# A gated graph network and three graph layers on one core: sums written into PSUM before the convolutions, one accumulator for both gates, GpSimd left with the split of x

## The reference, cut to what matters

```python
h = x                                              # layer 0: gated graph network, 3 steps
for _ in range(3):
    a = adj @ h                                    # in and out matrix are the same here
    av = concat([a, a])
    z  = sigmoid(av @ w3.T + w3_b + h @ u3.T + u3_b)
    r  = sigmoid(av @ w4.T + w4_b + h @ u3.T + u3_b)
    hv = tanh(av @ w5.T + w5_b + (r * h) @ u5.T + u5_b)
    h  = (1 - z) * h + z * hv
x = layernorm(x + h)
rel = adj.T * (q @ k.T)                            # layer 1: relation, rows divided by their norm
x = layernorm(x + (rel / norm(rel)) @ v)
x = layernorm(x + (adj @ x) @ l2_w + l2_bias)      # layer 2: first convolution
x = layernorm(x + (norm_adj @ x) @ l3_w + l3_bias) # layer 3: second convolution
```

## Time and profile before

| | |
|---|---|
| runs | 1341.83, 1343.10, 1343.95 us; median 1343.1 |
| profiled execution, span | 1341.3 us (its time is the span and some 1.8 us around it, by the median) |
| instructions | 21962 |
| PE matmul / weight load busy | 1283.5 us (96%) / 1130.6 us (84%) |
| DVE busy | 1074.2 us (80%) |
| ACT busy | 714.1 us (53%) |
| POOL busy | 530.3 us (40%) |
| granted TensorE clock | full in nearly all slices |

### The profile page before, as it was taken

The page is one execution under the profiler, slowest core; times in us unless marked ns, Lnnn a source line. Parts: engine busy times, 40 slices in busy tenths (PEclk is TensorE's granted clock), DMA queues, the critical chain, the costliest instruction groups (busy, mean ns, idle before and its releaser), DMA issues.

```text
span 1341.3 us, 21962 instructions
## 1 busy us (share of the span) xinstructions
PE 1283.5 (96%) x7912; PEld 1130.6 (84%) x7912; DVE 1074.2 (80%) x2110; ACT 714.1 (53%) x1229; POOL 530.3 (40%) x586
## 2 busy tenths in 40 slices
PE   7899999999999999999999999999999999999995
PEld 6788898888979889898888988889898888988795
DVE  5579788797878968788797887978789687885897
ACT  5655555545555555555555655455555555556541
POOL 1135343443443434443353444443534343441254
PEclk9999999999999999999999999999999999999998
DMA  5010100001000010000001001010000100000000
GB/s 173 1 32 1 40 10 16 31 0 47 0 20 27 0 47 0 31 16 16 31 0 47 0 16 31 0 47 0 31 16 0 47 0 31 16 16 1 1 1 32
DMA packets 29386, 29.19 MB, mean 22 GB/s; under 512 B 2352, under 2 KB 28464, under 8 KB 29360
## 3 DMA queue, kind: packets, MB, share of 16 engines
q1 hardware_dynamic: 27808, 28.32, 6.4%
q0 software_dynamic: 192, 0.52, 0.2%
q10 hardware_dynamic: 1360, 0.01, 0.1%
HBM read 20.45 MB, written 8.39 MB: 22 GB/s over the span
## 4 chain that ended last, share of the span: by engine, by line
PE 75%; DVE 14%; issue 5%; POOL 4%; DMA 1%; ACT 1%; DVEq 0%; ACTq 0%; POOLq 0%
PE b_ps L482 35%; PE f_ps L482 35%; DVE b_a_lo L1352 3%; POOL b_rstd L366 2%; PE f_ps L579 2%; DVE normed L1324 2%; DVE hb_feat L1285 2%; DVE b_a_lo L1259 1%; POOL b_var_eps L364 1%; PE b_ps L579 1%; PE b_ps L596 1%; DMA bias_in<-in_L_gnn_u_b 1%; DVE f_cand L1279 1%; PE b_ps L627 1%; DVE hb_node_lo L1299 1%
## 5 line engine op out<-in xcount | busy, mean ns | idle before, releaser
L364 POOL TENSOR_TENSOR b_var_eps<-b_moments,eps 128x2 f32<-128x2 f32 x120 | 34.6, 288 | 339.4 <-DVE b_moments L1313 339.3
L350 POOL TENSOR_TENSOR f_kept<-f_kept,hf_feat 128x512 f32<-128x512 f32 x66 | 91.0, 1379 | 169.7 <-ACT f_kept L941 169.6
L1324 DVE TENSOR_SCALAR normed<-summed,b_moments,b_rstd 128x256 f32<-128x256 f32 x180 | 96.5, 577 | 6.5 <-POOL b_rstd L366 6.5
L375 POOL TENSOR_TENSOR skip<-normed,bias_out 128x512 f32<-128x512 f32 x60 | 88.1, 1469 | 10.3 <-DVE normed L1324 10.3
L366 POOL TENSOR_TENSOR b_rstd<-b_var_eps,neg_half 128x2 f32<-128x2 f32 x120 | 86.1, 718 | 9.4
L350 POOL TENSOR_TENSOR b_kept<-b_kept,hb_feat 128x512 f32<-128x512 f32 x30 | 45.7, 1525 | 110.5 <-ACT b_kept L941 110.5
L1306 DVE BATCH_NORM_STATS2 b_stats<-summed 128x6 f32<-128x256 f32 x240 | 88.4, 410 | 0.8 <-issue 0.3
L946 ACT ACTIVATE f_cand<-f_ps,bias_c 128x512 f32<-128x512 f32 x66 | 45.5, 690 | 63.8 <-PE f_ps L482 63.5
L890 ACT ACTIVATE f_a_hi<-f_ps 128x512 fp32r<-128x512 f32 x68 | 40.6, 598 | 71.6 <-PE f_ps L482 69.9
L890 ACT ACTIVATE b_rh_hi<-b_ps 128x512 fp32r<-128x512 f32 x90 | 53.6, 596 | 45.4 <-PE b_ps L482 45.4
L482 PE MATMUL f_ps<-adjT_hi,hf_node_hi 128*128 128x256 f32 x264 | 75.8, 287 | 0.3 <-POOL hf_node_lo L338 0.3
(11 more groups left out here) (330 smaller groups left out, 5081.6 us busy)
## 6 DMA issues: line engine op xcount, KB each, us to landing
x_front<-in_x SPq DMA_DIRECT2D x16, 512.0 KB, 3.5
x_back<-in_x SPq DMA_DIRECT2D x15, 512.0 KB, 3.5
out<-result SPq DMA_DIRECT2D x15, 512.0 KB, 3.0
x_back<-in_L_gnn_u_w SPq DMA_DIRECT2D x2, 256.0 KB, 9.2
bias_out<-in_L_gnn_bias POOLq DMA_DIRECT2D x4, 128.0 KB, 6.7
b_z<-in_L_gnn_w_w SPq DMA_DIRECT2D x1, 512.0 KB, 11.6
b_gate<-in_L_gnn_w_w SPq DMA_DIRECT2D x1, 512.0 KB, 12.5
b_kept<-in_L_gnn_w_w SPq DMA_DIRECT2D x1, 512.0 KB, 13.0
```

Source lines behind the costliest of these rows:

```text
L350: pool.tensor_tensor(L.kept[:, k], L.kept[:, k], L.state.feat[:, k], ALU.mult).then_inc(L.s_kept, 1)
L364: pool.tensor_tensor(Y.var_eps[:, g], Y.moments[:, g, :, 1], eps[:], ALU.add).then_inc(Y.s_var, 1)
L375: pool.tensor_tensor(Y.skip[:, g], Y.normed[:, g], bias_out[:, j], ALU.add).then_inc(Y.s_skip, 1)
L1324: last = dve.tensor_scalar(dst[:, g, c], Y.summed[:, g, c], Y.moments[:, g, c, 0:1], Y.rstd[:, g, c:c + 1], ALU.subtract, ALU.mult)
```

## The change

- **Convolutions.** `fill` (DVE) writes normed + bias into ps0 ahead of `convolve`, whose matmuls then all accumulate onto it (start=False). `sum_conv`, `add_bias`, `skip` are gone; for layer norms 2 and 3 `stats_of` and `normalise` read ps0.
- **Gates.** `reset` accumulates w4 a onto ps0 itself; `reset_gate` takes the sigmoid from ps0 with its bias. `update` then adds (w3 - w4) a onto the same ps0, so it waits for the reset sigmoid. `keep_base` and `reset_arg` are gone; the matrix `w3 - w4` costs one subtraction on DVE at the start.
- **1 - z.** `keep_gate` is gone; DVE makes (z - 1) h with one scalar_tensor_tensor, and `new_h` subtracts it.
- **Norms.** The squares are summed on DVE and go to PE as plain fp32, two `pe.matmul` a graph in place of four; `squares_hi`, `squares_lo` are gone.
- **GpSimd** keeps the split of x, `inverse_std` and `inverse_norm`.
- All `body` and `finish` lists are written in a new order.

```diff
-                product(L.ps1[:, k], columns(w4T, k), mixed(L)).then_inc(L.s_reset, 1)
+                product(L.ps0[:, k], columns(w4T, k), mixed(L), start=False).then_inc(L.s_reset, 1)
...
             def update(L, n, k):
-                pe.wait_ge(L.s_a_lo, upto(n))
-                pe.wait_ge(L.s_base_kept, upto(n, k))
-                product(L.ps0[:, k], columns(w3T, k), mixed(L), start=False).then_inc(L.s_update, 1)
+                pe.wait_ge(L.s_r, upto(n, k))
+                product(L.ps0[:, k], columns(w34T, k), mixed(L), start=False).then_inc(L.s_update, 1)
...
             def candidate_mixed(L, n, k):
-                pe.wait_ge(L.s_reset_arg, upto(n, k))
+                pe.wait_ge(L.s_a_lo, upto(n))
...
                 if L is back and later(n):
-                    pe.wait_ge(main.s_sum, ln(n - 1, 3, k))
+                    pe.wait_ge(main.s_normed, ln(n - 1, 3, k))
...
-                pe.wait_ge(Y.s_sq_lo, upto(q, g))
+                pe.wait_ge(Y.s_sq_sum, upto(q, g))
                 for c in range(C):
-                    for part in (Y.sq_hi, Y.sq_lo):
-                        last = pe.matmul(Y.ps1[:, g, 2 * c:2 * c + 2], part[:, g, c * P:(c + 1) * P], ones[:],
-                                         start=part is Y.sq_hi, stop=part is Y.sq_lo, skip_group_check=True)
+                    last = pe.matmul(Y.ps1[:, g, 2 * c:2 * c + 2], Y.sq_sum[:, g, c * P:(c + 1) * P], ones[:],
+                                     start=True, stop=True, skip_group_check=True)
...
             def convolve(Y, q, j, g):
+                pe.wait_ge(Y.s_filled, conv(q, j, g))
                 pe.wait_ge(Y.s_ax_lo, conv(q, j, g))
                 for c in range(C):
                     last = product(Y.ps0[:, g, c * D:(c + 1) * D], graph_columns(Y.y_hi, Y.y_lo, g, c),
-                                   whole((w2s, w3s)[j]))
+                                   whole((w2s, w3s)[j]), start=False)
...
             def reset_gate(L, n, k):
-                act.wait_ge(L.s_reset_arg, upto(n, k))
-                act.activation(L.gate[:, k], L.gate[:, k], ACT.Sigmoid).then_inc(L.s_r, 1)
+                act.wait_ge(L.s_reset, upto(n, k))
+                act.activation(L.gate[:, k], L.ps0[:, k], ACT.Sigmoid, bias=bias_r[:, k:k + 1]).then_inc(L.s_r, 1)
...
+            def keep(L, n, k):
+                dve.wait_ge(L.state.s_feat, upto(n, k))
+                dve.wait_ge(L.s_z, upto(n, k))
+                dve.scalar_tensor_tensor(L.kept[:, k], L.z[:, k], 1.0, L.state.feat[:, k], ALU.subtract,
+                                         ALU.mult).then_inc(L.s_kept, 1)
...
-                dve.tensor_tensor(dst[:, k], L.kept[:, k], L.cand[:, k], ALU.add).then_inc(done, 1)
+                dve.tensor_tensor(dst[:, k], L.cand[:, k], L.kept[:, k], ALU.subtract).then_inc(done, 1)
...
+            def layer_sum(Y, j, g, c):
+                return Y.summed[:, g, c] if j < 2 else Y.ps0[:, g, c * D:(c + 1) * D]
...
-            def sum_conv(Y, q, j, g):
-                dve.wait_ge(Y.s_skip, conv(q, j, g))
-                dve.wait_ge(Y.s_conv, conv(q, j, g))
-                dve.tensor_tensor(Y.summed[:, g], graph_bank(Y.ps0, g), Y.skip[:, g], ALU.add).then_inc(Y.s_sum, 1)
+            def fill(Y, q, j, g):
+                dve.wait_ge(Y.s_normed, ln(q, j + 1, g))
+                dve.tensor_tensor(graph_bank(Y.ps0, g), Y.normed[:, g], bias_out[:, j], ALU.add).then_inc(Y.s_filled, 1)
```

The new order of the body on PE (the calls that moved; f is `front`, b is `back`, 2p is the first and 2p+1 the second step):

```diff
                 update(back, q, 0)
+                for k in range(2):
+                    mix(front, 2 * p, k, p)
                 candidate_mixed(back, q, 0)
                 update(back, q, 1)
                 candidate_mixed(back, q, 1)
                 for k in range(2):
                     candidate_reset(back, q, k)
-                for k in range(2):
-                    mix(front, 2 * p, k, p)
                 base(front, 2 * p, 0)
+                reset(front, 2 * p, 0)
                 turn_h3(main, q, 0)
                 base(front, 2 * p, 1)
+                reset(front, 2 * p, 1)
+                update(front, 2 * p, 0)
+                turn_x1(main, q, 0)
                 turn_h3(main, q, 1)
```

More of the change, by code:

```diff
@@ L726, in finish @@
                 turn_input(LAST, 0)
-                mix(back, LAST - 1, 0)
+                for k in range(2):
+                    mix(back, LAST - 1, k)
                 turn_input(LAST, 1)
-                base(back, LAST - 1, 0)
-                mix(back, LAST - 1, 1)
+                for k in range(2):
+                    base(back, LAST - 1, k)
                 for k in range(2):
@@ L745, in finish @@
-                base(back, LAST - 1, 1)
+                for k in range(2):
+                    candidate_reset(front, 2 * LAST, k)
+                for k in range(2):
+                    reset(back, LAST - 1, k)
                 for k in range(2):
                     turn_h(state_f, 2 * LAST + 1, k)
+                candidate_mixed(back, LAST - 1, 0)
                 update(back, LAST - 1, 0)
-                base(front, 2 * LAST + 1, 0)
                 for k in range(2):
                     mix(front, 2 * LAST + 1, k)
-                update(back, LAST - 1, 1)
@@ L774, in finish @@
+                update(front, 2 * LAST + 2, 0)
+                turn_h3(main, LAST - 1, 1)
                 for k in range(2):
[L775 to L778 removed]
+                    candidate_mixed(front, 2 * LAST + 2, k)
+                update(front, 2 * LAST + 2, 1)
                 turn_x1(main, LAST - 1, 0)
[L780 removed]
@@ L1114, in finish @@
[L1114 to L1123 removed]
+                node_hi(state_f, 2 * LAST + 1, 0, 2 * LAST + 0 + 1)
@@ L1199, in _ @@
                 rh_hi(front, 0, k)
-            for k in range(C):
-                keep_gate(front, 0, k)
                 update_gate(front, 0, k)
@@ L1211, in _ @@
             for k in range(C):
-                keep_base(front, 1, k)
-            for k in range(C):
                 a_hi(front, 1, k)
@@ L1218, in _ @@
                 rh_hi(front, 1, k)
-            for k in range(C):
-                keep_gate(front, 1, k)
                 update_gate(front, 1, k)
@@ L1668, in _ @@
                 prep_lo(i, prep_bank(i))
-            for k in range(C):
-                reset_arg(front, 0, k)
             for k in range(C):
@@ L1683, in _ @@
             for k in range(C):
+                keep(front, 0, k)
                 candidate_part(front, 0, k)
@@ L1698, in _ @@
             for k in range(C):
-                reset_arg(front, 1, k)
-            for k in range(C):
                 reset_h(front, 1, k)
@@ L1711, in _ @@
             for k in range(C):
+                keep(front, 1, k)
                 candidate_part(front, 1, k)
```

736 lines of the change are left out of this document (312 added, 424 removed).

## The result

The changed kernel takes **1309.5 us** (median of 4 runs, 1309.20 to 1310.19) against 1342.5 us of the kernel before beside it (1341.64 to 1343.95). The ratio is 0.9754, with a 95% interval of 0.974 to 0.9768: 2.5% faster, 33 us, where 42 were forecast.

The account below looks back on a forecast made before the run. PE was taken as the bound, with only its stalls and own work changeable. 1341.3 - 38.7 + 1.8 - 5.0 + 0 = 1299.4 us, plus 1.8 around it: 1301 us; range 1291 to 1320, likeliest case's own 1293 to 1308.

Parts of the forecast that it names:

- The stalls and their cause: PE waits 2.8 us a body for late DVE results, because GpSimd's large instructions stretch DVE's with both operands in SBUF.
- The third stall: 0.41 us lost ahead of `reset` of `back`, behind the normalisation of `result`, stretched by GpSimd's split of x.
- 14 x 2.29 + 13 x 0.51 = -38.7: All PE stalls in the loop bodies go, so a body takes 78.4 us: -38.7 us.
- second `mix_nodes` of convolution 1: Place of the 0.77 us stall: input at T+72.7, PE there at T+73.4, so in time.
- the walk: One body stepped through with the new lists, T the start of `turn_input`; every input in time for PE.
- The price of PSUM operands: `normalise` of layer norms 2 and 3 reads PSUM: up to +0.26 us for each of four pairs; low end taken.
- the second rival: Small stalls at `turn_h` of `back` and second `mix_nodes`, 0.5 to 1 us a body: 1308 to 1315 us; chance 0.2.
- The norms: Two fp32 matmuls a graph, four instructions as before, 0.11 us each: cost 0, upper end +17 us.
- the third rival: The norms' fp32 matmuls cost their upper end, 0.24 us apart: +17 us, 1318 us; chance 0.08.
- The start: Ahead of the loop, three DVE instructions, 0.6 us apart, are put on the path: +1.8 us.
- The end: In `finish()`, DVE stretching and one `sum_conv` go: at least 2.3 us, at most 10 or so; -5 taken.
- The fifth rival: GpSimd's split of x comes late for the first `mix` of `front`, making the kernel slower; chance 0.06.

Follow-up runs that it names:

- Experiment 4: Kernel before with keep and add_bias, GpSimd's ten large instructions a body, moved to DVE and nothing else changed: 1348.56 us, ratio 1.0044.
- Experiment 3: Changed kernel with ten unused GpSimd additions of 512 elements a body, started by the events that started keep or add_bias: 1400.62 us, ratio 1.0434.
- Experiment 11: Changed kernel with a 32-byte tensor, a swapped DVE pair and early keep, plus the second convolution's first fill moved behind conv_ax_lo: 1298.28 us.
- experiment 7: Changed kernel with an unused 32-byte tensor and the second convolution's lo part put ahead of the first half of hand_over_h: 1302.52 us.

## Why the prediction was right, and where it was short

**The stalls and their cause**: right. Experiment 4 shows it best: with GpSimd's ten instructions gone and ten more on DVE, the stretched rows have their short times and the stall at the second `mix_nodes` is gone. Experiment 3 brings the stretched rows back with additions that nobody reads, though about half of the growth of its longest stall is GpSimd's queue. The third stall is as the prediction had it, without a row shown for it; here it is, and ahead of it the reverse, a GpSimd instruction of 0.20 us stretched to 0.53 beside one of DVE:

```profile
223.34 0.66 DVE L1294 TENSOR_TENSOR hb_feat_lo<-hb_feat,hb_feat_hi 128x512 fp32r<-128x512 f32 x1
223.52 0.53 POOL L364 TENSOR_TENSOR b_var_eps<-b_moments,eps 128x2 f32<-128x2 f32 x1
...
224.84 1.29 POOL L338 TENSOR_TENSOR hf_node_lo<-x_front,hf_node_hi 128x512 fp32r<-128x512 f32 x1
224.91 1.70 DVE L1324 TENSOR_SCALAR result<-summed,b_moments,b_rstd 128x256 f32<-128x256 f32 x2 [0.26 <-POOL b_rstd L366]
```

One sentence of the prediction was too narrow: not only instructions "with both operands in SBUF" stretch. `normed` and `result` have one large operand there, and went from 0.73 to 1.71 and 1.70 us a pair. The same section of the Trainium skill ("SBUF — State Buffer", Who interferes with whom) has it that a DVE instruction with at most one SBUF input and outside its two-port modes doesn't contend. The 1.00 us of `normed` from PSUM amid GpSimd's additions agrees. That quiet on GpSimd would be enough was never the sum's claim, and experiment 4 shows that it isn't.

**14 x 2.29 + 13 x 0.51 = -38.7**: the mechanism was right, the size was not. Measured -27.5. Of the 11.2 us,
- 5.9 are the offset of the tensors: with the old places a body takes 78.78 us and not 79.20, 14 x 0.42. The term "everything else in a body is PE at the pace of its instructions" took the old pace for granted. No row of the kernel before could have given this.
- 4.8 are the wait that was left, 14 x 0.34, at a place on the prediction's list of places where PE comes soon: "second `mix_nodes` of convolution 1: T+72.7 against T+73.4". In the body that starts at 139.98 the lo part ends at T+73.86, 1.16 late by the walk, and PE would have come at T+73.67. The walk had 0.73 us for the pair of `normed`; it takes 1.00. And it had 1.1 us from the end of the moments to the normalisation by way of GpSimd; from the start of GpSimd's first instruction alone it is 1.73 us (208.71 to 210.44), beside DVE instructions with two SBUF operands. The walk looked at what GpSimd does to DVE and never at the reverse, which the kernel before already showed (the 0.53 above). A hop between engines priced too low is what the prediction named as its weak point. Experiment 11 moves `fill` off the place: the two instructions have their short times and the wait goes, while the pair of `normed` stays at 0.99.
- The last 0.5 us lie in the first body, which takes 80.50 us. It was to take 79.27, by 81.56 before and the 2.29 of its stalls; 0.77 of the difference are the two items above. For the rest see the granted clock, the third number from the end, right behind the start of the first body, here and in experiment 7:

```profile
59.50:62.00 2.50, 2.50 (x13) 2.39 (x12) 1.38 (x3) 0.60 (x1) 0.00 (x0) 0.50 0.00 0
...
59.25:62.00 2.75, 2.05 (x18) 1.81 (x17) 1.66 (x3) 0.83 (x2) 0.00 (x0) 1.00 0.00 0
```

At the end of the start PE waits 2.91 us for a new h, and in this run the clock is then 1.2 GHz up to 62 us. In the kernel before the same happens behind a wait of 2.40 us, from 56.4 to 59.4, for the most part still ahead of the loop. In experiment 7 the wait is 2.91 us too and the clock stays full; PE waits 0.70 us for `hb_node_lo` there instead, and the first body takes 79.61 us. So the last 0.5 us are mostly a slow stretch that fell into the first body, and no part of the change decides where it falls.

**The price of PSUM operands**: the low end was taken, 0, "because the two rows of the pair stand in unlike places". They did not mislead: 1.00 against 0.73 is +0.27, the upper end by the +0.26 of the earlier trace rows. It was this that the Trainium skill ("VectorE: DVE Perf Modes", Why PSUM operands drop a tier) spoke for. By it the second rival was to be the outcome. A small stall did come, and the price of PSUM is a part of it, but at 0.34 us a body and not 0.5 to 1. That the time (1309.5) is nearer to this rival's 1308 to 1315 than to the forecast's 1301 is luck: the stall alone is 4.8 us, and with the old places of the tensors the same instructions take 1303.2, within the forecast's own 1293 to 1308. `keep` cost nothing more than a tensor_tensor: 0.68 us.

**The norms**: 0 forecast, 0 measured, 0.09 us a record; the third rival is out.

**The start** +1.8, measured +1.3. The work was priced right: the last transposes ahead of the loop start at 56.38 us before and at 58.17 after, 1.8 later. The other 0.5 is the clock again, since those transposes up to the loop's start took 1.77 us before and 1.31 after. **The end** -5.0, measured -7.9: it was bounded and not walked, and the value was set too near to the lower bound. These two give back 3.4 us. (The low end of the range is called the sum with -13 for the end; that sum is 1293, not 1291, and -13 lies beyond the "10 or so" given as the bound. Nothing hangs on it.)

**The sum**: 1299.4 - 0.5 + 11.2 - 2.9 = 1307.2, the span; 2.3 us around it in place of 1.8 give 1309.5. The time lies within the range and 1.5 us outside the likeliest case's own, and would lie further out if the end hadn't given 2.9 us more than forecast.

**The fifth rival** (GpSimd's split of x is late): no sign of it. All 60 instructions of the split lie between 1.28 and 1.31 us, beside a DVE that reads PSUM there.

## What to carry to other kernels

When an instruction of VectorE or GpSimd takes longer than its like elsewhere, look at what the other of the two runs at that moment, in both directions: beside a large one on GpSimd a VectorE instruction with two SBUF operands took up to 1.77 us in place of 0.68, and beside two such VectorE instructions in a row the tiny pair on GpSimd, on whose result the chain waits, took 1.70 us (208.71 to 210.41) in place of 0.97 (206.21 to 207.18). Reading from PSUM costs 0.27 us a pair here, and in the rows shown such an instruction wasn't stretched; where the two engines meet, from SBUF it cost 1.0 us a pair. And before a difference of half a per cent is put down to an edit, move the tensors by 32 bytes and measure again: here the allocation alone was worth 5 to 8 us. The same care goes for a single profile: an extra microsecond behind a long wait can be the granted clock of that one execution, so read the clock column there first.
